# A graph network kernel on one core: first ranked segment of 6 chunks instead of 8, and node rows loaded behind the given rows

## The chip, the cores and the metric

The kernel runs on 1 core of one Trainium2 chip. The metric is the device time of one execution, in microseconds (us): the median of the runs of a kernel. Engines are named as in the profile: PE (matmul), DVE (VectorE), ACT (ScalarE), POOL (GpSimd), SP (SyncE). SPq, ACTq and POOLq are the DMA-issuing instructions of an engine.

## The reference

Four message-passing layers over one graph of 3125 nodes with 160 features and 100000 edges. Each layer normalises the node rows, gathers one node row per edge, multiplies it with edge weights from a small network on the edge's attributes, and sums the products per node; a dense stage per node follows. In outline:

```python
edge_index = jnp.stack([src, dst])
h = jnp.maximum(_layernorm(x, axis=-1), 0.0)
x = x + _L0_gnn_ref(h, edge_attr_3, edge_attr_64, ..., edge_index)   # gathers h[dst], sums per src
h = jnp.maximum(_layernorm(x, axis=-1), 0.0)
x = x + _L1_gnn_ref(h, node_vec1, src, dst, edge_attr_4, edge_attr_10, ...)  # gathers h[src], sums per dst
...
return x
```

Layer 0 sums over `src`, which arrives unsorted, so the edges have to be brought into bins of `src` first. Layers 1 to 3 sum over `dst`, which arrives sorted. Everything that the change touches lies in this ordering stage ahead of layer 0.

## The kernel before

**What the ordering stage does.** The edges lie as 128 partitions by 782 columns, cut into 34 chunks of 23 columns. `src` falls into 100 bins of 32 nodes. Each edge needs a slot of `rows_dram[0]` (tiles of 128 edges, each within one bin). The stage has these parts:

- *Init.* ACT issues one DMA (`rows_a<-acc`, line 997) that fills the whole of `rows_dram[0]` with blank rows; it signals `s_init`. POOL waits for it ahead of its first scatter (line 787), SP ahead of the rows below (line 596).
- *Count and rank, on DVE and PE.* `count(0)` marks each of the 100 bins over all 782 columns and PE sums the marks; `bases(0)` makes each column's base. `rank(o, lo, hi)` then makes, for the columns lo to hi, one mark per bin (line 1261), two matmuls on PE (lines 1814 to 1817) and one predicated copy on DVE (line 1400). `positions` turns the ranks into slots (lines 1410 to 1415) and signals `s_pos[0]`. Ranking runs in three segments, `SEGMENTS = (0, 8, 18, 34)` in chunks: segment 0, then `vectors(1, ...)` (unit vectors of the columns behind segment 0; those of segment 0 are made within `count(0)`), `tiles(0)`, segment 1, `count(1)`, `bases(1)`, `tiles(1)` (whose end is line 1375, `s_out_rows`), `turn_keys`, segment 2 and two halves of `rank(1)`. The statistics of the node rows wait for `s_nodes` behind all of that.
- *Scatter, on POOL.* For each chunk, 23 indirect DMAs (line 794), one per column, write one edge row per partition to its slot. A chunk needs its rows staged in one of two buffers (`stage_rows`, SP, line 572, waits until the scatter two chunks earlier has landed) and filled by ACT (`fill`, lines 1040 to 1046: vector, index, key, slot).
- *Given rows.* The second set of edge attributes goes in given order from DRAM through SBUF, where ACT adds two columns (`complete`, lines 1010 and 1012), back to DRAM (`given`, SP, lines 579 and 583), 34 chunks through two buffers. SP does 35 steps of it: a step loads chunk c and stores chunk c-1.

**The order of SP's queue** is written by hand and is what the change edits: key and vector loads, `stage_rows` 0 and 1, the node rows `x` and `attr` (lines 587 and 590, signal `s_nodes`), the `src` keys a second time (lines 593, 595), the wait for `s_init`, then 11 steps of `given`, `stage_rows(2)`, and `GIVEN_EACH` = 4 steps between each later `stage_rows` up to chunk 7, then the steps that are left. Behind these: a wait for `s_out_rows`, five small tables written out (lines 669 to 673), a wait for the given rows' stores, `tile_starts` written, waited for and read back (lines 679 to 681), and only then `stage_rows` of the first chunk of segment 1:

```python
sp.dma_start(starts_dram[:, :], starts_row[0:1, :]).then_inc(s_blocks, 16)
sp.wait_ge(s_blocks, 16)
sp.dma_start(block_at[0:ROW_GROUPS, :], ...).then_inc(s_blocks, 16)
...
for c in range(SEGMENTS[1], CHUNKS):
    stage_rows(c, c // 2, c % 2)
```

**The order of ACT's queue** follows it: fills of the chunks of segment 0 with 10 and then `GIVEN_EACH` `complete`s between them, after `roots(1)`, the square roots of `vectors(1, ...)`.

Behind the last scatter the edge stage of layer 0 begins: SP waits for `s_scat`, DVE for `s_placed`.

Of the kernel before, what the change touches and what calls it, by code (L numbers as in the profile page):

```python
# [16 lines left out]
P = 128  # L17
# [3 lines left out]
BLOCKS = -(-NODES // P)  # L21
# [13 lines left out]
CHUNKS = COLS // CHUNK  # L35
# [16 lines left out]
ENDS = (0, 6, 12, 18, 22, BLOCKS)  # L52
R2, R3 = math.sqrt(2.0), math.sqrt(3.0)
assert COLS % CHUNK == 0 and CHUNKS % 2 == 0 and GROUPS % 2 == 0
SEGMENTS = (0, 8, 18, CHUNKS)
BLOCKS_FROM = 10
BLOCK_LANES = 64
BLOCK_STEPS = GT * (P // BLOCK_LANES)
GIVEN_FIRST, GIVEN_EACH = 10, 4
assert BLOCKS_FROM >= SEGMENTS[1] + 2 and BLOCKS_FROM % 2 == 0 and BLOCKS_FROM + BLOCK_STEPS + 2 <= CHUNKS  # L60
assert GIVEN_FIRST + GIVEN_EACH * (SEGMENTS[1] - 2) == CHUNKS
ROW_GROUPS = TCOLS * P // GT
# [4 lines left out]
assert WORK >= 2 * PRODS * 416 + 2 * 512  # L67
PREP_FROM = SEGMENTS[2]
VEC_CUTS = (0, SEGMENTS[1] * CHUNK, COLS)
PAD_STEP = NODES // (P * GT)  # L70
# [17 lines left out]
def within(v, n):  # L88

    return not is_static(v) or 0 <= v < n  # L90
# [9 lines left out]
def wait(eng, signal, value):  # L100

    if is_static(value) and value <= 0:
        return
    if isinstance(signal, Signal):
        eng.wait_ge(signal.sem, value + signal.base)
    else:
        eng.wait_ge(signal, value)
# [127 lines left out]
def gnn_program(nc, t):  # L235

    ctx = ExitStack()
    with ctx:
        def sb(name, shape, dt=F32):
            return ctx.enter_context(nc.sbuf_tensor(name, shape, dt))  # L240

        def sem(name):
            return ctx.enter_context(nc.semaphore(name))
# [15 lines left out]
        x = sb("x", [P, BLOCKS * NF])  # L259
        attr = sb("attr", [P, BLOCKS])  # L260
# [131 lines left out]
        s_nodes = sem("s_nodes")  # L392
# [149 lines left out]
        def block_buffer():  # L542

            return gath_flat[0:ROW_GROUPS, 0:BLOCK_LANES * B_W]

        def pair_record(kind, i):

            _, record = nc.values_load_multi_w_load_instructions(
                guide[0:1, bass.ds(i * RECORD, RECORD)], engines=(kind,), min_val=0, max_val=COLS - 1,
                skip_runtime_bounds_check_because="bins and columns of tiles")  # L550
            bins = [nc.s_assert_within(v, 0, BINS - 1, skip_runtime_bounds_check_because="bins") for v in record[0:2]]
            return bins + list(record[2:4])
# [9 lines left out]
        def _(sp):  # L562
# [5 lines left out]
            def stage_rows(c, half, q):  # L568

                wait(sp, s_scat[q], half * (16 * CHUNK))  # L570
                sp.sem_inc(s_apart["sp"], 1)
                sp.dma_start(stage[0][q], t["rows_a"][:, bass.ds(c * (CHUNK * A_W), CHUNK * A_W)]).then_inc(s_stage[0][q], 16)

            def given(c, half, q):

                if within(c, CHUNKS):
                    wait(sp, s_given[q], half * 16)
                    sp.sem_inc(s_apart["sp"], 1)
                    sp.dma_start(stage[1][q], t["rows_b"][:, bass.ds(c * (CHUNK * B_W), CHUNK * B_W)]).then_inc(s_stage[1][q], 16)
                if within(c - 1, CHUNKS):  # L580
                    wait(sp, s_fill[1], c * 2)
                    sp.sem_inc(s_apart["sp"], 1)
                    sp.dma_start(given_dram[0:P * COLS, :].rearrange("(p c) w -> p (c w)", p=P)[:, bass.ds((c - 1) * (CHUNK * B_W), CHUNK * B_W)],
                                 stage[1][1 - q]).then_inc(s_given[1 - q], 16)
            for c in range(2):
                stage_rows(c, 0, c)
            sp.dma_start(x[:, :].rearrange("p (j c) -> p j c", j=BLOCKS),
                         t["x"].rearrange("(j p) c -> p j c", p=P)).then_inc(s_nodes, 16)
            with nc.allow_non_contiguous_dma(reason="one word per node"):
                sp.dma_start(attr[:, :], t["node_vec1"].rearrange("(j p) c -> p (j c)", p=P)).then_inc(s_nodes, 16)  # L590

            whole = COLS // P * P
            sp.dma_start(flat_keys[:, 0:whole].bitcast(I32).rearrange("p (b e) -> p b e", e=P),
# [3 lines left out]
            step = 0  # L597
            for c in range(2, SEGMENTS[1]):
                for _ in range(GIVEN_FIRST + 1 if c == 2 else GIVEN_EACH):
# [2 lines left out]
                stage_rows(c, c // 2, c % 2)  # L602
            for step in range(step, CHUNKS + 1):
                given(step, step // 2, step % 2)

            def tables(n, parts):

                S, m = s_p[n], BLOCKS // STORES
                for i in parts:
                    wait(sp, S["h"] if n == 2 else S["tab"], m * (i + 1))  # L610
                    sp.dma_start(table_dram[n].rearrange("(j p) c -> p j c", p=P)[:, m * i:m * (i + 1), :],
                                 table[:, m * i * NF:m * (i + 1) * NF].rearrange("p (j c) -> p j c", j=m)).then_inc(S["td"].sem, 16)
# [70 lines left out]
            def store_block(i):  # L683
# [3 lines left out]
                             block_buffer().rearrange("g (l c) -> g l c", c=B_W)).then_inc(s_copy, 16)  # L687
            for c in range(SEGMENTS[1], CHUNKS):
                stage_rows(c, c // 2, c % 2)
# [37 lines left out]
        def _(pool):  # L727
# [88 lines left out]
            for q in range(2):  # L816
                pool.wait_ge(s_scat[q], 16 * CHUNK * (CHUNKS // 2))

            pool.wait_ge(s_copy, 16 * BLOCK_STEPS)
            pool.wait_ge(s_flag, 1)  # L820
            _, (flag,) = nc.values_load_multi_w_load_instructions(
                unsorted[0:1, 0:1], engines=(POOL,), min_val=0, max_val=P * COLS,
                skip_runtime_bounds_check_because="a count of edges")
            with pool.If(flag != 0):
# [27 lines left out]
                with pool.Fori(0, TCOLS * P // GT) as c:  # L852
                    _, start = nc.values_load_multi_w_load_instructions(
                        starts_row[0:1, bass.ds(c * GT, GT)], engines=(POOL,),
                        min_val=0, max_val=P * COLS, skip_runtime_bounds_check_because="clamped to the number of edges")
                    for w in range(GT):
                        pool.dma_start(tiles_b[:, bass.ds(c, 1), w, :], sorted_dram[bass.ds(start[w], P), :].unsqueeze(1)).then_inc(s_gd, 16)
                    pool.wait_ge(s_gd, c * (16 * GT) + (ordered + 16 * GT))
                    pool.sem_inc(s_apart["pool"], 1)
# [1220 lines left out]
```

## Time and profile before

| what | us |
|---|---|
| median of 3 runs | 5577.6 (5576.04 to 5580.81) |
| the profiled execution, its own time | 5567.3 |
| its span in the trace | 5564.6 |
| POOL busy over the span | 4003.2 (72%) |
| DVE busy | 3534.9 (64%) |
| PE busy | 4312.1 (77%) |

Times in the trace count from the start of the span. Of the profiled execution 2.7 us lie outside its span. "Idle before" an instruction is followed by what released it; 0.30 us with the releaser "issue" is the gap between two instructions of one engine that wait for nothing. In a timeline row the columns are start, duration, engine, line, operation, operands, count, and in brackets the idle time before it.

### The profile page before, as it was taken

Reading aid. Unit: us, or ns where it says so; the run is one execution under the profiler, and the core shown is the slowest. Engines: PE = TensorE matmul, PEld = TensorE weight load, DVE = VectorE, ACT = ScalarE, POOL = GpSimd, SP = SyncE. Lnnn points to the kernel's source line nnn. Section 1 sums busy time; section 2 is a strip of 40 time slices with the busy share of each in tenths; the row PEclk is TensorE's granted clock in tenths of the full one; section 3 lists DMA queues with packets and bytes.
Section 4 is the critical chain, followed back from the end, with each engine's and each line's share of the span. In section 5 each row is a group of like instructions: output and inputs, shape, how many; then the busy total and the mean of one; then the engine's idle time right before and its main releaser. Section 6 shows DMA issues by size and latency. Waiting matters only on the chain.

```text
span 5564.6 us, 105356 instructions
## 1 busy us (share of the span) xinstructions
PE 4312.1 (77%) x24426; PEld 3347.2 (60%) x24426; DVE 3534.9 (64%) x11475; ACT 3407.4 (61%) x14606; POOL 4003.2 (72%) x4336
## 2 busy tenths in 40 slices
PE   7796112089999999889999997555566788889998
PEld 5553011067777777777888886444444576667777
DVE  8896000177777777667778887333333477778888
ACT  0000000056666666378899997677788778888896
POOL 5777777777777777377777775777777557777775
PEclk9898555599999999999999998555555699999999
DMA  9624553144444444133333331333333223333332
GB/s 317 183 82 105 126 121 89 53 90 95 94 93 94 94 94 92 28 81 80 81 81 82 83 82 53 81 79 82 80 81 82 63 63 81 80 82 82 82 83 52
DMA packets 632977, 504.27 MB, mean 91 GB/s; under 512 B 424231, under 2 KB 538342, under 8 KB 630455
## 3 DMA queue, kind: packets, MB, share of 16 engines
q0 software_dynamic: 183824, 307.52, 22.0%
q1 hardware_dynamic: 430566, 156.52, 12.2%
q10 hardware_dynamic: 17984, 33.56, 1.6%
q8 instruction: 212, 3.47, 0.3%
q14 instruction: 391, 3.20, 0.2%
HBM read 400.41 MB, written 96.88 MB: 89 GB/s over the span
## 4 chain that ended last, share of the span: by engine, by line
POOL 29%; issue 22%; PE 22%; DVE 4%; DMA 2%; POOLq 1%; DVEq 1%; ACT 0%; SPq 0%; ACTq 0%
POOL gath L961 24%; PE bank L1948 6%; PE bank L1922 4%; POOL gath L939 4%; PE bank L1950 4%; PE bank L1998 2%; PE bank L1990 1%; DVE acc L1529 1%; PE bank L1944 1%; PE bank L1892 1%; DMA gath<-table,acc 1%; DMA gath<-table,rows 1%; DVE work L1563 1%; POOLq L952 1%; DVE work L1545 0%
## 5 line engine op out<-in xcount | busy, mean ns | idle before, releaser
L961 POOL DMA_INDIRECT gath<-table,acc x2346 | 2223.5, 948 | 763.9 <-issue 691.2
L1121 ACT ACTIVATE sel<-acc,rows 128x32 f32<-128x32 f32 x10560 | 2293.0, 307 | 434.2 <-DVE acc L1520 431.0
L1529 DVE TENSOR_TENSOR acc<-acc,bank 128x160 f32 (+1 forms) x3520 | 1213.5, 345 | 942.3 <-PE bank L1944 561.8
L1948 PE MATMUL bank<-work,sel 128*128 128x160 f32 (+1 forms) x5280 | 1400.2, 347 | 116.3 <-DVE acc L1529 111.6
L1950 PE MATMUL bank<-work,sel 128*128 128x160 f32 x5280 | 1154.4, 300 | 0.0
L1948 PEld LDWEIGHTS bank<-work,sel 128*128 128x128 f32 x5280 | 838.6, 190 | 401.0 <-issue 382.9
L939 POOL DMA_INDIRECT gath<-table,rows x880 | 840.4, 955 | 278.4 <-issue 247.7
L1922 PE MATMUL bank<-w,work 64*128 64x224 f32 (+2 forms) x5280 | 921.1, 369 | 49.2 <-DVE work L1545 42.7
L794 POOL DMA_INDIRECT rows_a<-acc x782 | 754.5, 965 | 281.8 <-issue 237.8
L1950 PEld LDWEIGHTS bank<-work,sel 128*128 128x128 f32 x5280 | 913.2, 191 | 45.8
L1944 PE MATMUL bank<-gath,sel 128*128 x1760 | 566.3, 496 | 411.3 <-POOLq L947 357.1
L1944 PEld LDWEIGHTS bank<-gath,sel 128*128 128x128 f32 x1760 | 442.3, 315 | 535.2 <-issue 517.7
L1922 PEld LDWEIGHTS bank<-w,work 64*128 64x128 f32 (+1 forms) x5280 | 558.7, 188 | 311.8 <-issue 234.8
L1542 DVE TENSOR_TENSOR work<-bank,gath 128x128 f32<-128x128 f32 x1760 | 503.1, 286 | 212.5 <-POOLq L947 131.3
L1545 DVE TENSOR_TENSOR work<-bank,gath 128x192 f32<-128x192 f32 x1760 | 610.0, 347 | 4.0 <-issue 3.1
L1121 ACT ACTIVATE sel<-sel,rows 128x32 f32<-128x32 f32 x2640 | 581.8, 309 | 43.4 <-DVE sel L1520 41.4
L1040 ACT ACTIVATE acc<-acc 128x69 f32 (+1 forms) x34 | 9.3, 272 | 850.9 <-DMA acc<-in_rows_a 768.1
L1105 ACT ACTIVATE work<-bank 128x512 f32<-128x512 f32 (+1 forms) x330 | 241.8, 733 | 272.0 <-PE bank L1892 232.6
L1563 DVE TENSOR_TENSOR work<-bank,gath 128x288 f32<-128x288 f32 x880 | 356.8, 447 | 0.0
L1817 PE MATMUL bank<-acc,ident 100*128 100x391 f32 (+3 forms) x1000 | 346.6, 438 | 0.0
L1745 PE MATMUL bank<-ident,sel 128*64 128x128 f32 x25 | 10.2, 408 | 404.1 <-ACT sel L1023 404.1
L1559 DVE TENSOR_TENSOR work<-bank,gath 128x256 f32<-128x256 f32 x440 | 184.9, 420 | 152.1 <-POOLq L927 137.9
(288 smaller groups left out, 3646.7 us busy)
## 6 DMA issues: line engine op xcount, KB each, us to landing
rows<-rows_b SPq DMA_DIRECT2D x330, 128.0 KB
gath<-table,acc POOLq DMA_INDIRECT x2346
rows_a<-acc ACTq DMA_DIRECT2D x1, 30360.0 KB, 103.6
rows<-rows_a SPq DMA_DIRECT2D x110, 256.0 KB
acc<-in_rows_a SPq DMA_DIRECT2D x34, 793.5 KB, 7.3
rows_b<-gath SPq DMA_DIRECT2D x16, 896.0 KB, 10.5
gath<-table,rows POOLq DMA_INDIRECT x880
acc<-in_rows_b SPq DMA_DIRECT2D x34, 368.0 KB, 3.7
```

The costliest lines, as they stand in the source:

```text
L794: pool.indirect_dma_start(rows_dram[0][:, :], bass.IndirectOffsetOnAxis(ap=pos_r[q][:, u:u + 1], axis=0), stage[0][q][:, u * A_W:(u + 1) * ...
L939: pool.indirect_dma_start(gath[q][:, u, :], None, table_dram[n][:, :], bass.IndirectOffsetOnAxis(ap=at, axis=0)).then_inc(S[f"gt{k % LANES ...
L961: pool.indirect_dma_start(gath_all[:, u, :], None, table_dram[n][:, :], bass.IndirectOffsetOnAxis(ap=index[:, k:k + 1], axis=0)).then_inc( ...
L1121: i = act.activation(sel[q][:, t, at:at + BIN], hot, ACT.Copy, scale=e[:, k:k + 1])
L1529: dve.tensor_tensor(sums, sums, bank(6 + b, P, 256 * h, 256 * h + L.width), ALU.add).then_inc(S["fl"].sem, 1)
L1542: dve.tensor_tensor(ps, wt[:, 0:128].rearrange("p (w c) -> p w c", w=2), one[:, 0:S0].unsqueeze(1).to_broadcast([P, 2, S0]), ALU.mult)
L1545: ins = dve.tensor_tensor(pv, wt[:, 128:L.wcols].rearrange("p (w m) -> p w m", w=nv) .unsqueeze(2).to_broadcast([P, nv, 3, V1]), one[:, S0 ...
L1563: ins = dve.tensor_tensor(pv, wt[:, h, 128:L.wcols].rearrange("p (w m) -> p w m", w=nv) .unsqueeze(2).to_broadcast([P, nv, 3, V1]), two[:, ...
L1922: ins = pe.matmul(bank(at_bank, P, first, first + L.wcols), hid, w, start=True, stop=True, skip_group_check=True)
L1944: ins = pe.matmul(out, sel[qv][:, t, 0:128], ring_column(columns[h]), start=True, stop=True, skip_group_check=True)
L1948: pe.matmul(out, sel[qv][:, t, 96:224], work[:, a + NF:a + NF + L.width], start=True, stop=False, skip_group_check=True)
L1950: ins = pe.matmul(bank(6 + b, P, 256 * h, 256 * h + NF), sel[qv][:, t, 0:128], work[:, a:a + NF], start=False, stop=True, skip_group_check ...
```

## The change

The first segment has 6 chunks instead of 8 and the second 12 instead of 10. `GIVEN_EACH` becomes 6, so that all 34 `complete`s still fit between the fills of segment 0. The two loads of node rows move from the head of SP's queue to behind the last step of `given`.

```diff
-SEGMENTS = (0, 8, 18, CHUNKS)
+SEGMENTS = (0, 6, 18, CHUNKS)
-GIVEN_FIRST, GIVEN_EACH = 10, 4
+GIVEN_FIRST, GIVEN_EACH = 10, 6
@@ sync engine
             for c in range(2):
                 stage_rows(c, 0, c)
-            sp.dma_start(x[:, :].rearrange("p (j c) -> p j c", j=BLOCKS),
-                         t["x"].rearrange("(j p) c -> p j c", p=P)).then_inc(s_nodes, 16)
-            with nc.allow_non_contiguous_dma(reason="one word per node"):
-                sp.dma_start(attr[:, :], t["node_vec1"].rearrange("(j p) c -> p (j c)", p=P)).then_inc(s_nodes, 16)
...
             for step in range(step, CHUNKS + 1):
                 given(step, step // 2, step % 2)
+            sp.dma_start(x[:, :].rearrange("p (j c) -> p j c", j=BLOCKS),
+                         t["x"].rearrange("(j p) c -> p j c", p=P)).then_inc(s_nodes, 16)
+            with nc.allow_non_contiguous_dma(reason="one word per node"):
+                sp.dma_start(attr[:, :], t["node_vec1"].rearrange("(j p) c -> p (j c)", p=P)).then_inc(s_nodes, 16)
```

## Rows read from the trace of the kernel before

**Rows 1.** Windows by stage; PE, PEld, DVE, ACT, POOL busy, PEclk, DMA share, GB/s.
```profile
107.60:1120.20 1012.60, 426.80 (x1702) 262.41 (x1702) 413.97 (x1116) 49.78 (x248) 769.57 (x798) 0.67 0.43 110
```

**Rows 2.** Waits of POOL, 0 to 1150 us: total, times, longest.
```profile
POOL rows_a L794 <- issue: 237.8, 780, 0.3
POOL rows_a L794 <- ACT acc L1046: 43.7, 1, 43.7
```

**Rows 3.** Timeline of POOL: first scatter, first of chunk 6, first of chunk 8.
```profile
107.60 1.26 POOL L794 DMA_INDIRECT rows_a<-acc  x1 [43.66 <-ACT acc L1046]
...
286.07 0.96 POOL L794 DMA_INDIRECT rows_a<-acc  x1 [0.30 <-issue]
...
344.56 0.96 POOL L794 DMA_INDIRECT rows_a<-acc  x1 [0.31 <-issue]
```

**Rows 4.** DMA issues, 0 to 120 us: count, KB each, us to landing.
```profile
rows_a<-acc ACTq DMA_DIRECT2D x1, 30360.0 KB, 103.6
```

**Rows 5.** Timeline of ACT: init DMA, fill of chunk 0, roots(1), fills of chunks 4, 8.
```profile
2.86 0.58 ACTq L997 DMA_DIRECT2D rows_a<-acc  x1
...
106.01 0.27 ACT L1040 ACTIVATE acc<-acc 128x69 f32<-128x69 f32 x1 [82.80 <-DVE acc L1415]
...
109.99 0.70 ACT L1002 ACTIVATE acc<-acc 128x598 f32<-128x598 f32 x1 [2.90 <-DVE acc L1273]
...
207.16 0.27 ACT L1040 ACTIVATE acc<-acc 128x69 f32<-128x69 f32 x1 [8.83 <-DMA acc<-in_rows_a]
...
321.59 0.21 ACT L1046 ACTIVATE acc<-acc 128x23 int32 x1
```

**Rows 6.** DMA queues, 16 to 41 us: packets, MB, share of 16 engines.
```profile
q10 hardware_dynamic: 3302, 7.29, 73.7%
q1 hardware_dynamic: 3300, 2.06, 26.0%
```

**Rows 7.** The same, 42 to 59 us: SP's queue (q10 has 2825 too).
```profile
q1 hardware_dynamic: 2825, 0.01, 9.9%
```

**Rows 8.** The same, 68 to 100 us.
```profile
q10 hardware_dynamic: 5522, 12.19, 105.8%
```

**Rows 9.** Windows: the 100 bins of segment 0, those of segment 1.
```profile
54.13:103.93 49.80, 48.38 (x304) 35.56 (x304) 47.81 (x201) 0.00 (x0) 7.63 (x15) 0.97 1.03 371
125.89:180.60 54.71, 52.89 (x300) 37.39 (x300) 52.75 (x200) 4.03 (x24) 41.59 (x44) 0.96 0.64 187
```

**Rows 10.** Timeline of SP's queue: node rows, then given rows, then chunks 2 to 8.
```profile
4.87 0.53 SPq L587 DMA_DIRECT2D x<-in_x  x1
5.44 24.32 SPq L590 DMA_DIRECT2D attr<-in_node_vec  x1
29.80 18.70 SPq L593 DMA_DIRECT2D side<-in_skey  x1
...
106.52 0.84 SPq L579 DMA_DIRECT2D acc<-in_rows_b  x2
...
157.59 0.37 SPq L572 DMA_DIRECT2D acc<-in_rows_a  x1
...
178.26 0.34 SPq L572 DMA_DIRECT2D acc<-in_rows_a  x1
...
199.93 0.87 SPq L572 DMA_DIRECT2D acc<-in_rows_a  x1
...
301.84 4.37 SPq L583 DMA_DIRECT2D rows_given<-acc  x2
...
316.23 117.19 SPq L572 DMA_DIRECT2D acc<-in_rows_a  x5
```

**Rows 11.** Timeline of DVE: end of tiles(1), s_out_rows.
```profile
247.25 0.42 DVE L1375 TENSOR_SCALAR acc<-acc 1x196 int32<-1x196 int32 x1
```

**Rows 12.** DMA, 5528 to 5531 us: one store of 640-byte rows alone, GB/s in 40 slices.
```profile
GB/s 0 34 196 316 375 341 375 350 333 384 367 333 375 350 367 367 358 358 375 333 188 43 17 17 0 0 0 0 0 0 0 0 0 0 0 0 0 0 0 0
```

**Rows 13.** DMA queues, 308 to 312 us: packets, MB, share of 16 engines.
```profile
q1 hardware_dynamic: 792, 0.02, 10.0%
```

## The prediction

> **What bounds the kernel now.** I read the windows by stage first. The change touches only the first 1120 us; behind them the same program runs as before. In the stage from 107.6 to 1120.2 us POOL is busy for 770 of 1013 us and everything else far less [rows 1]. The waits of POOL say why that is the bound: its scatters were never late. 780 of the 782 scatters show only the fixed gap of 0.30 us, and one wait, of 43.7 us, stands ahead of the first [rows 2]. So the stage is "start of the first scatter, plus 1012 us of POOL", and the edge stage of layer 0 waits for its end. Two things can move the time: the start at 107.60 us, and any chunk that comes to POOL late [rows 3]. There the reader is to see also where chunk 6, the first one behind the new segment 0, begins (286.07), and chunk 8, the first one behind the old (344.56).
>
> **What sets the start.** Two chains end at the same moment. The init DMA is issued at 2.86 us and lands 103.6 us later, at 106.5 [rows 4, 5]; SP's first given rows go out at 106.52, just behind it [rows 10]. DVE has the positions of segment 0 at 105.8, ACT's fill begins at 106.01 and ends at 106.6 [rows 5]. POOL starts 1.0 us behind the later one. Each half of the change shortens one of the two chains, so they have to be costed together.
>
> **The init chain.** While x loads, the init's queue (q10) and SP's (q1) move packets one to one: 3302 and 3300 in 25 us, or 132 per us each [rows 6]. With nothing beside it the init moves 5522 in 32 us, 172.6 per us [rows 8]. The 3200 rows of x take 24.2 us at 132 per us, and cost the init 24.2 x (1 - 132/172.6) = 5.7 us. While attr loads (3200 packets of one word, 2825 in 17 us, 166 per us, 19.3 us in all) the init loses 19.3 x (1 - 166.2/172.6) = 0.7 us [rows 7]. Without both it lands 6.4 us earlier, at 100.1.
>
> **The DVE chain.** The 100 bins of segment 0 take 49.8 us at 184 columns, those of segment 1 54.7 at 230, DVE being busy for 96% of both [rows 9]. The trace has no 138 columns; carried on by the same step of 46 columns that is 44.9, 4.9 us less (bounds: nothing, if the pitch of a bin had its floor at 184 columns, and 12.5, if the time went with the columns; I take the step, being the nearest rows). The unit vectors of 138 columns instead of 184 inside count(0) and the shorter position steps save an estimated 1.1 us. Positions stand at 99.8, the fill's end at 100.6. Segment 1 has 276 columns instead of 230 and gives the 4.9 us back; tiles(1) still ends near 248 us [rows 11], which is early enough for everything below.
>
> POOL therefore starts at 101.5, **6.1 us earlier**. If nothing came late that would be the whole result.
>
> **The supply of chunks 2 to 6.** Here the same edit adds to SP's queue. Its waits let the order count: 11 given steps take from 106.52 to 157.59, then chunk 2 is staged; 4 steps and a stage take 20.7, then 21.7 us, so a step is 5.1 us [rows 10]. All of this moves with the init, plus 0.7 us, since roots(1), which now has two chunks' more vectors and a start later against the init, holds the first complete [rows 5]. With 6 steps between stages: chunk 2 is staged at 100.1 + 0.7 + 51.1 = 151.9, chunk 3 at 182.8 (20.7 + 10.2 later), chunk 4 at 214.7 and chunk 5 at 246.6 (31.9 each). From a staging to the start that it allows pass 7.5 to 8.8 us: chunk 4, staged at 199.93, was filled from 207.16 for 0.6 us [rows 5, 10], and POOL takes its 1.0. POOL wants them at 161, 191, 221 and 251 us: its six chunks ahead of chunk 6 took 178.5 us [rows 3], 29.7 each. Chunks 4 and 5 come late by some 2 us each; a cycle of 31.9 us can't feed a chunk of 29.7. POOL would want chunk 6 at 284.3: of the 6.1 us gained about 4 are gone by then.
>
> **Chunk 6 is the large term.** It isn't staged within the given rows but behind them and behind tile_starts, as chunk 8 was. Before, the pair of given stores that ended the stream was through SP's queue at 306.2, the last of them issued at 305.8, and chunk 8's rows at 316.23, so 10.4 us lie between: the tables, the landing of tile_starts and its way back [rows 10]. Its fill ended at 321.8 [rows 5], while POOL wanted it at 344.6 [rows 3]: 22.8 us to spare, which hid all of it. Now two chunks less stand ahead of it, 58 us of POOL, and the given rows end only 29 us earlier, at 246.6 + 30.3 = 276.9 (6 steps). Behind them come x and attr, and tile_starts lands behind both, being on the same queue.
>
> What x and attr cost there the trace doesn't show, since they ran beside the init. x: 640-byte rows alone move at about 355 GB/s [rows 12], which gives 5.8 us for 2.05 MB [rows 6]; beside the init it took 24.2; I take 6, the nearer case, with nothing but scatters beside it. attr: from below, 1.7 us, the 9.9% share of 17 us that its packets held of the engines [rows 7]; from above, 19.3 us, its pace one to one with the init. The nearest row is the store of the two-word records, 792 packets in 4 us on a queue that was else nearly idle [rows 13]: 16.2 us for 3200. That one has other gaps in it (three issues one behind another), so I take 11, between it and the pace at which 640-byte rows run (5.8). The 24.32 us that attr's issue took before [rows 10] I take for the queue being full beside the init, not for work of SP: x's packets moved at 132 per us then, and 24.32 us of that are its 3200.
>
> The Trainium skill ("DMA: Bandwidth & Descriptors", the fit in "Anatomy of one DMA") prices a DMA at 2.0 us plus bytes over 436 GB/s, by size alone. By that fit x would be 6.7 us and attr 2.0, and the sum 8 us smaller than mine. That the pair's drain depends on attr's count of packets is what I set against it; no row of before shows attr alone.
>
> **Sum.** Chunk 6 staged at 276.9 + 10.4 + 6 + 11 = 304.3; filled 5.6 us later, started after 1.0 more: 310.9. Before it started at 286.07. Net **+24.8 us**, with a stall of 26.6 us at chunk 6 that swallows the gain at the front and the two small stalls. Chunk 7 is staged right behind 6; from chunk 8 on a stage waits for the scatter two chunks back and has a whole chunk's time, as before. The 782 scatters themselves, the gathers between them and all that follows keep their time. Against the profiled execution that is 5567.3 + 24.8 = 5592.1; the median of the runs stands 10.3 us above it, so 5602.4.
>
> At nothing I cost the wait of statistics for s_nodes: x and attr land near 300 us, and DVE comes to it beyond 500 us. If that cover were gone it would delay the table of layer 0, not the scatters.
>
> **Rivals.**
> - *Small packets are cheap.* attr takes its lower bound, 1.7 us, and chunk 6 is 9.3 us earlier: +15.5, 5593. For it: the packets hardly slowed the init. Against it: the records' pace. Chance 0.22. The skill's fit says the same (+16 or so).
> - *SP itself is held.* The 24.32 us of attr and the 18.70 us of the issue behind it [rows 10] are SP's own work in making descriptors, not a full queue. Then the tables go out 43 us later instead of 17 and the sum is +51, 5628. Against it: x, with as many packets, was issued in 0.53 us. Chance 0.06.
> - *The supply keeps up* (the faster side). The place is the given stream: if a given step took 4.3 us or less instead of 5.1, the 34 steps up to the last store would save 27 us, chunk 6 would be ready when wanted, and 6.1 us would stay: 5571. It decides from a staging of chunk 6 at 277 us or before, which is where I put the end of the given rows, without the 27 us behind it. For it: the first steps run ahead of the scatters' full load, and the loads alone land in less. Against it: a step waits for a store to land and for ACT, so each costs its latency whatever runs beside it, and the first eleven took 51.1 us [rows 10], 4.6 each, with no stage between them. Chance 0.04.
> - *Both ends kind*: a pace of 4.9 and a cheap attr give +9, 5587, within 0.2%. Chance 0.09.
> - My forecast, attr at 6 to 19 us: 0.59.
>
> **Numbers.** 0.2% is 11 us, about what a measurement of this kernel can tell from no change. The range takes attr from 1.7 to 19.3 us (+15.5 to +33) and 2 to 3 us for the pace of the given steps on either side, and a little of the held SP: 5589 to 5615. Slower by over 0.2%: 0.59 + 0.22 + 0.06 less a little, 0.86; within 0.10; faster 0.04.
>
> **What the next profile would show.** Right: the first scatter at about 101.5 us; the init landing near 100; small waits of POOL ahead of chunks 4 and 5 and one of 20 to 35 us ahead of chunk 6, then none; the last scatter at about 1144 us; behind it nothing changed. In SP's queue the last given store near 277 and the first staging of segment 1 near 304. Wrong: no wait at chunk 6 (the queue is faster than I read it), a first scatter still at 107 (a third chain holds it), or a change behind 1120 us.

## The result and the profile after

| | before | after |
|---|---|---|
| median, 6 runs each (us) | 5577.9 (5576.0 to 5580.8) | 5612.6 (5610.0 to 5613.6) |
| the profiled execution, its own time | 5567.3 | 5610.0 |
| its span | 5564.6 | 5608.4 |
| first scatter | 107.6 | 125.2 |
| first scatter of chunk 6 | 286.1 | 321.1 |
| first scatter of the last chunk | 1091.4 | 1128.3 |

The change makes the kernel 34.7 us slower, a ratio of 1.0061 (1.0049 to 1.0072). The forecast was 5602.4 with a range of 5589 to 5615. In two of the five sets of runs below every execution, those of the kernel before among them, took about 7800 us for a reason that no run shows; up to the end of segment 0 their traces run as the others do (in the segments alone the first scatter is at 125.0 there and at 124.8 in the other set), and the argument uses only that part of them.

The two profiled executions differ by 43.8 us in span: 37.3 up to the end of the scatters, and 6.5 behind it, where the program is the same and single executions of the kernel before already differ by up to 13.5 us (5567.3 to 5580.8).

The first view is again the windows by stage, of the kernel after: the 100 bins of segment 0, and the stage from the first scatter to the last (columns as in [rows 1]).

```profile
53.44:120.80 67.36, 66.95 (x299) 59.43 (x300) 46.93 (x200) 0.00 (x0) 7.49 (x15) 0.50 0.72 261
125.20:1157.50 1032.30, 437.43 (x1702) 262.28 (x1702) 425.52 (x1116) 50.06 (x248) 773.49 (x798) 0.67 0.43 109
```

The stage of the scatters is 20 us longer than before (1032 for 1013 us in [rows 1]), and it starts 17.6 us later. Segment 0, which has a quarter fewer columns, takes 67.4 us where it took 49.8 [rows 9]: PE is busy for 66.95 of the 67.36 us, DVE no longer is, and the granted clock is 0.50 throughout where it was 0.97. That row is what the forecast didn't see.

The waits of POOL in the kernel after, 0 to 1180 us, and its timeline at chunks 0, 5 and 6, answer to [rows 2, 3].

```profile
POOL rows_a L794 <- issue: 236.9, 777, 0.5
POOL rows_a L794 <- ACT acc L1046: 74.8, 4, 58.4
```

```profile
125.21 1.41 POOL L794 DMA_INDIRECT rows_a<-acc  x1 [58.43 <-ACT acc L1046]
...
276.69 1.41 POOL L794 DMA_INDIRECT rows_a<-acc  x1 [0.95 <-ACT acc L1046]
...
321.11 0.96 POOL L794 DMA_INDIRECT rows_a<-acc  x1 [15.10 <-ACT acc L1046]
```

So two places carry the loss: chunk 6, as forecast, though its wait is 15.1 us and not 26.6, and the start, which was to be 6 us earlier and is 17.6 later. Behind chunk 6 come 1.9 us more by the last chunk. Chunk 5 was late by 0.95 us, and a fourth wait holds the 0.3 that are left of the 74.8.

SP's queue of the kernel after answers to [rows 10].

```profile
101.22 0.82 SPq L579 DMA_DIRECT2D acc<-in_rows_b  x2
128.96 0.34 SPq L583 DMA_DIRECT2D rows_given<-acc  x1
...
172.52 0.37 SPq L572 DMA_DIRECT2D acc<-in_rows_a  x1
...
205.86 0.35 SPq L572 DMA_DIRECT2D acc<-in_rows_a  x1
...
236.92 0.37 SPq L572 DMA_DIRECT2D acc<-in_rows_a  x1
...
267.71 0.37 SPq L572 DMA_DIRECT2D acc<-in_rows_a  x1
...
293.80 4.37 SPq L583 DMA_DIRECT2D rows_given<-acc  x2
298.21 0.43 SPq L601 DMA_DIRECT2D x<-in_x  x1
298.69 6.77 SPq L604 DMA_DIRECT2D attr<-in_node_vec  x1
...
312.16 0.23 SPq L679 DMA_DIRECT2D tile_starts<-acc  x1
314.84 0.31 SPq L681 DMA_DIRECT2D acc<-tile_starts  x1
315.28 0.85 SPq L572 DMA_DIRECT2D acc<-in_rows_a  x2
```

And the DMA issues, the first row of 0 to 125 us, the others of 297 to 315 us (KB each, us from issue to landing):

```profile
rows_a<-acc ACTq DMA_DIRECT2D x1, 30360.0 KB, 98.3
```

```profile
x<-in_x SPq DMA_DIRECT2D x1, 2000.0 KB, 10.7
...
attr<-in_node_vec SPq DMA_DIRECT2D x1, 12.5 KB, 12.2
```

Three things stand in them. The init lands after 98.3 us, not 103.6: the first given rows go out at 101.2, 5.3 us earlier, where 6.4 were forecast. But the first of them is stored only at 128.96, since ACT's `complete` stands behind `roots(1)`, which waits for segment 0. And attr's issue takes 6.8 us, not 24.3. x lands 10.7 us after its issue, at 308.9, and attr 12.2 us after its own, at 310.9.

**Where the clock went.** Windows of the stretch around the start of the ranking, first of the kernel before, then of the kernel after. From 49 to 53 us PE has almost nothing to do, as it waits for DVE's bases; 58 to 100 is ranking.

```profile
49.00:53.00 4.00, 0.82 (x6) 0.36 (x4) 2.85 (x8) 0.00 (x0) 1.60 (x4) 1.00 1.09 376
53.00:58.00 5.00, 3.46 (x14) 2.87 (x15) 3.79 (x15) 0.00 (x0) 2.51 (x5) 0.67 1.09 374
58.00:100.00 42.00, 41.74 (x272) 30.38 (x271) 41.66 (x177) 0.00 (x0) 5.12 (x11) 1.00 1.06 384
```

```profile
49.00:53.00 4.00, 0.34 (x2) 0.25 (x2) 3.36 (x9) 0.00 (x0) 3.21 (x7) 1.00 1.04 367
53.00:58.00 5.00, 4.15 (x20) 3.73 (x20) 3.71 (x17) 0.00 (x0) 0.00 (x0) 0.52 1.05 378
58.00:100.00 42.00, 42.00 (x189) 37.27 (x188) 29.65 (x125) 0.00 (x0) 7.49 (x15) 0.50 0.99 358
```

Both kernels lose the full clock (2.4 GHz) just behind that pause. Before, it is at half from 54.7 to 58.1 us and comes back. After, it is at half (1.2 GHz) from 53.2 to 148.8 us: through the whole of segment 0, although PE is busy for 42.00 of 42 us, and through the pause of 17.6 us behind it. It comes back 4.0 us after segment 1, with its 276 columns, begins on PE:

```profile
139.79 3.14 PE L1794 MATMUL bank<-ident,acc 128*1 128x128 f32 x14 [17.64 <-DVE acc L1339]
144.82 0.41 PE L1816 MATMUL bank<-work,acc 128*128 128x276 bf16 x1 [1.89 <-DVE work L1261]
```

The groups of PE by shape between 60 and 95 us, line 1817 in the kernel before and in the kernel after, give the price of a matmul (busy us, mean ns; neighbours overlap, so the busy time is less than count times mean):

```profile
L1817 PE MATMUL bank<-acc,ident 100*128 100x184 f32 x152 | 35.2, 334 | 0.0
```

```profile
L1817 PE MATMUL bank<-acc,ident 100*128 100x138 f32 x106 | 35.9, 486 | 0.0
```

With fewer columns the matmul takes 486 ns for 334. In DVE's timeline of the kernel after, the copies now stand 0.67 us apart, each waiting for PE (before they stood 0.47 apart with no wait):

```profile
95.12 0.32 DVE L1400 COPY_PREDICATED acc<-work,bank 128x138 f32<-128x138 int16 x1 [0.20 <-PE bank L1817]
95.33 0.25 DVE L1261 TENSOR_SCALAR work<-acc,iota_bins 128x138 bf16<-128x138 bf16 x1
95.79 0.32 DVE L1400 COPY_PREDICATED acc<-work,bank 128x138 f32<-128x138 int16 x1 [0.20 <-PE bank L1817]
```

A hundred bins of 0.67 us are the 67 us of segment 0. Behind the scatters nothing changed: 4420 us from just behind their end, after and then before, hold the same work to within 1%.

```profile
1150.00:5570.00 4420.00, 3765.72 (x21997) 2991.51 (x21998) 2992.47 (x9929) 3347.38 (x14299) 3167.64 (x3417) 0.88 0.33 80
```

```profile
1113.00:5533.00 4420.00, 3779.09 (x22053) 3007.04 (x22054) 2998.60 (x9955) 3346.18 (x14312) 3163.84 (x3419) 0.88 0.33 80
```

### The profile page after: what moved, and what is told of

It reads as the page before. It is cut to its first block, busy times and chain, and to the rows that moved or that the text cites. A ratio compares the mean times of both kernels' runs of the same rounds, so it can differ in the third digit from the quotient of the medians.

```text
span 5608.4 us, 105367 instructions
## 1 busy us (share of the span) xinstructions
PE 4333.8 (77%) x24426; PEld 3361.4 (60%) x24426; DVE 3546.1 (63%) x11475; ACT 3412.2 (61%) x14606; POOL 4015.8 (72%) x4336
## 3 DMA queue, kind: packets, MB, share of 16 engines
q1 hardware_dynamic: 430566, 156.52, 12.2%
## 4 chain that ended last, share of the span: by engine, by line
POOL 29%; issue 22%; PE 20%; DVE 5%; DMA 1%; DVEq 1%; POOLq 1%; SPq 0%; ACT 0%; ACTq 0%
POOL gath L961 24%; PE bank L1948 6%; POOL gath L939 4%; PE bank L1922 4%; PE bank L1950 4%; PE bank L1998 2%; DVE acc L1529 2%; PE bank L1990 1%; PE bank L1944 1%; DMA gath<-table,acc 1%; PE bank L1892 1%; DVE work L1563 1%; DVE work L1545 1%; DVE work L1542 1%; POOLq L952 1%
## 5 line engine op out<-in xcount | busy, mean ns | idle before, releaser
L1817 PE MATMUL bank<-acc,ident 100*128 100x391 f32 (+3 forms) x1000 | 375.6, 473 | 0.0
L1745 PE MATMUL bank<-ident,sel 128*64 128x128 f32 x25 | 10.2, 406 | 411.3 <-ACT sel L1023 411.3
## 6 DMA issues: line engine op xcount, KB each, us to landing
rows_a<-acc ACTq DMA_DIRECT2D x1, 30360.0 KB, 98.3
```

## The experiments

Three questions. Which half of the change costs what? Why is the clock at half in segment 0: because its bins are now too narrow in themselves (W), or because the pause takes the clock away and something has to bring it back (B)? And if B, what brings it back? Last: with both causes mended, is there a faster kernel?

### The two halves alone

The segments alone: the kernel after, with the two loads of node rows back at the head of SP's queue.

```diff
@@ sync engine, kernel after
                 stage_rows(c, 0, c)
+            sp.dma_start(x[:, :]..., t["x"]...).then_inc(s_nodes, 16)
+            sp.dma_start(attr[:, :], t["node_vec1"]...).then_inc(s_nodes, 16)
...
                 given(step, step // 2, step % 2)
-            sp.dma_start(x[:, :]..., t["x"]...).then_inc(s_nodes, 16)
-            sp.dma_start(attr[:, :], t["node_vec1"]...).then_inc(s_nodes, 16)
```

> The change without its second part: SEGMENTS (0, 6, 18) and 6 given steps between stagings, node rows loaded at the head of SP's queue as before. Theory W (the narrow rank): 138 columns a bin leave PE too little to do, its granted clock falls to half at the end of count(0) and stays there, so segment 0 takes 67 us as in the changed kernel, first scatter at 125 us, the init's landing (106) hidden behind it. Chunk 6 is staged 10.4 us behind the last given store instead of 17.5, so 7 us less than the changed kernel: 5605 us. Rival P (the clock's fall is due to the node rows' move or to chance): clock back to full within a few us as before, first scatter at 107.6, chunk 6 at about 300: 5592 us.

> The kernel of e1_segments_only again, for its time on a chip on which the kernel before takes about 5570 us. x and attr at the head of SP's queue, so chunk 6 is staged 10.4 us behind the last given store and not 17.5: 7 us less than the changed kernel's +34.7, +28 against before, 1.0050. First scatter at 125 as in the changed kernel. Rival: x and attr cost nothing behind the given rows, +35.

The first of these runs belongs to a 7800-us set: 7839.8 against 7813.7 us, 1.0026 (1.0003 to 1.0049), with the clock at half from 52.8 to 148.4 us and the first scatter at 125.0. The second: 5604.5 against 5581.3, **1.0039 (1.0025 to 1.0053), +23 us** where 28 were expected. The clock is at half from 52.5 to 148.1 and the first scatter at 124.8. So the late start belongs to the segments alone and has nothing to do with the loads. In its SP queue the last given store ends at 292.9 and chunk 6 is staged 9.2 us behind it; POOL waits 4.8 us for chunk 6, where the kernel after waits 15.1. Of the 13.2 us by which chunk 6 is staged earlier than there the loads explain 7.9. The other 5.3 come from the given rows, which end that much earlier here (292.9 against 298.2); the expected 28 didn't have them, and no run explains them.

```profile
288.43 4.50 SPq L583 DMA_DIRECT2D rows_given<-acc  x2
292.98 0.81 SPq L669 DMA_DIRECT2D tile_guide<-acc  x1
...
302.12 5.94 SPq L572 DMA_DIRECT2D acc<-in_rows_a  x2
```

The move alone: the kernel after with the old segments.

```diff
-SEGMENTS = (0, 6, 18, CHUNKS)
+SEGMENTS = (0, 8, 18, CHUNKS)
-GIVEN_FIRST, GIVEN_EACH = 10, 6
+GIVEN_FIRST, GIVEN_EACH = 10, 4
```

> The other part alone: node rows behind the given rows, SEGMENTS (0, 8, 18) and 4 given steps as before. Theory W: segment 0 at 184 columns keeps its clock, positions at 105.8, so DVE's chain holds the first scatter at 107 although the init lands at 101. Chunk 8 had 22.8 us to spare and x and attr cost 7 of them: no wait. 5577 us, within 0.1% of before. Rival P: the clock stays at half once the node rows are gone from the head, segment 0 takes 80 us or more, first scatter beyond 135: 5605 us.

> The kernel of e2_move_only again, for its time on such a chip. Init lands at 101 instead of 106.5, but DVE's chain holds the first scatter at 107 to 108; x and attr lie behind the given rows, where chunk 8 had 22.8 us to spare: no change, within 1 us of before. Rival: up to 5 us faster, if the init alone held the start.

7824.6 against 7813.7 us, 0.9998 (0.9971 to 1.0024), in the 7800-us set, and 5580.7 against 5581.3, **0.9999 (0.9989 to 1.0008)**, in the other. The init lands earlier and gains nothing, since segment 0 with its 184 columns holds the first scatter (at 109.0; in the first run 108.1); the 8.7 us that the loads add behind the given rows are hidden in the 22.8 to spare at chunk 8. The end of the given stores at 306.4 and the first staging at 325.11 are 18.7 us apart, for 10.0 before [rows 10]: that is the price of x and attr there, 8.7 us. The last chunk's first scatter is 3.4 us later than before (1094.9), which the time doesn't show. In both runs the clock comes back after some 7 us, though PE pauses as it does in the kernel after.

### Width or pause

Bridging the pause: the kernel after, with 14 matmuls of 128 columns on PE ahead of its wait for the totals and 5 behind the small matmul that follows, into a bank that nothing reads. The bins stay at 138 columns.

```diff
@@ tensor engine, bases(0)
+                if o == 0:
+                    for _ in range(14):
+                        pe.matmul(bank(3, P, 0, P), ident[:, :], tri, start=True, stop=True, ...)
                 pe.wait_ge(s_total, o + 1)
                 pe.matmul(bank(2, BINS, 0, 1), ...).then_inc(s_first, 1)
+                if o == 0:
+                    for _ in range(5):
+                        pe.matmul(bank(3, P, 0, P), ident[:, :], tri, start=True, stop=True, ...)
```

> The changed kernel with 14 matmuls (128x128 f32, result unused) on PE while it waits for bases(0), and 5 behind the first-slot product: PE has no pause before segment 0. Theory W: full clock to about 54 us, and it falls all the same within segment 0, since the bins are as narrow: segment 0 over 60 us, first scatter at 115 to 125, time 5605 to 5613. Rival B (the pause alone is to blame; at 138 columns a clock that never fell stays up): full clock through segment 0, 45 us for it, first scatter at 102, chunk 6 at about 301, 5592 us.

> The kernel of e3_bridge_pause again, for its time on a chip on which the kernel before takes about 5570 us. From e3 (first scatter at 103.0, clock full through segment 0) and from the changed kernel (17.5 us between last given store and chunk 6's staging): given rows end near 274, chunk 6 is staged near 292 and starts near 298 where POOL wants it at 281.5: +12 us against before, 1.0021. Rival: with the start mended chunk 6 is no longer late, and the time is 4 us below before.

The first run (7813.9 against 7813.7 us, 0.9999, 0.9975 to 1.0022) showed the clock at full from 16.7 to 98.7 us and the first scatter at 103.0. The second: 5577.0 against 5570.7, **1.0014 (1.0005 to 1.0024), +6.3 us** where 12 were expected, since the given rows end at 269.0 and not near 274; the clock is at full from 14.1 to 99.5. Its windows over the same three stretches, and its waits of POOL:

```profile
49.00:53.00 4.00, 3.58 (x33) 3.38 (x31) 3.36 (x12) 0.00 (x0) 0.25 (x1) 1.00 1.05 369
53.00:58.00 5.00, 4.82 (x41) 4.41 (x41) 4.97 (x25) 0.00 (x0) 2.23 (x5) 1.00 1.04 379
58.00:100.00 42.00, 36.79 (x266) 29.14 (x264) 40.92 (x184) 1.08 (x8) 5.45 (x11) 0.99 0.98 357
```

```profile
POOL rows_a L794 <- DMA rows_a<-acc: 39.0, 2, 38.7
POOL rows_a L794 <- ACT acc L1046: 11.7, 1, 11.7
```

Theory W falls: bins of 138 columns hold the full clock perfectly well once they have it, with PE less busy than in the kernel after (36.8 of 42 us). Entered at half, they don't get it back in the six other traces with 138 columns. The bins take 42.7 us from the first matmul at 53.18 to the last copy at 95.84, DVE-bound, and POOL now waits for the init's landing (the releaser is the DMA `rows_a<-acc`), not for positions. What is left against the kernel before is the wait of 11.7 us at chunk 6.

### What brings the clock back

More work per bin: the kernel after, with one more matmul of 64 columns, with weights of its own, behind each bin of segment 0.

```diff
@@ tensor engine, rank
                               start=False, stop=True).then_inc(s_prefix, 1)
+                    if o == 0 and lo == 0:
+                        pe.matmul(bank(3, P, 0, 64), ident[:, :], tri[:, 0:64], start=True, stop=True, ...)
```

> The changed kernel with one more matmul per bin of segment 0 (128x128 by 64 columns f32, result unused), so that PE has as much to stream per bin as at 184 columns; the pause stays. Theory W: the clock falls in the pause and comes back within some 4 us as in the kernel before, a bin takes 0.42 to 0.45 us, first scatter at 102 to 104, chunk 6 at about 301 us since x and attr and the given rows hold it: 5592 us. Rival B or P: half clock stays, the added matmul costs 0.2 us more per bin, first scatter at 145, time 5632 us.

The expectation that the clock would come back was wrong: 7872.2 against 7813.7 us, 1.0072 (1.0045 to 1.0099). The clock stays at half from 53.0 to 182.7 us, and the first scatter moves out to 156.7. Its window from 58 to 100 us has PE and its weight loads both at 42.00 of 42 us:

```profile
58.00:100.00 42.00, 42.00 (x212) 42.00 (x212) 19.83 (x85) 0.00 (x0) 3.55 (x8) 0.50 0.99 357
```

Wider matmuls: the kernel after, in which PE alone ranks 184 columns in segment 0. DVE still marks and copies 138, and what PE computes beyond them is read by nobody.

```diff
-            def rank(o, lo, hi):
+            def rank(o, lo, hi, wide=0):
 
+                hi += wide
...
-            pe.wait_ge(s_base[0], 1)
-            rank(0, 0, SEGMENTS[1] * CHUNK)
+            pe.wait_ge(s_base[0], 2)
+            rank(0, 0, SEGMENTS[1] * CHUNK, 2 * CHUNK)
```

> The changed kernel with PE ranking 184 columns in segment 0 as before the change, while DVE marks and copies 138 (PE streams 46 columns more per matmul, results unused; it starts one base later). The pause stays. Theory C (what counts for the clock's return is how much PE streams per bin without more weight loads): clock at half at 53, full again some 4 to 7 us later, first scatter at 103 to 104. Rival D (it is DVE's shorter work or the instant of the fall): clock stays at half, a bin takes PE 0.83 us, first scatter at 138 or later. Chunk 6 late as in the changed kernel under both: under C chunk 6 at about 298, 5590 us on a chip like that of the first profiles.

7789.8 against 7797.8 us, 0.9985 (0.9962 to 1.0008), in the 7800-us sets, so only its segment 0 is read. There the clock is at half for 3.4 us (54.0 to 57.4) and then full, as in the kernel before; the first scatter is at 102.8.

```profile
58.00:100.00 42.00, 40.59 (x288) 34.95 (x285) 41.00 (x193) 0.00 (x0) 3.64 (x9) 1.00 0.99 357
```

So adding a third more columns to the matmuls that are there, with no further weight load, makes the ranking *faster* (DVE's marks and copies untouched). More instructions on the same engine don't do it. Where the pause is left as it was, the clock comes back within 3.4 to 6.8 us in all four traces in which PE ranks 184 columns (the kernel before, the move alone twice, this one), and not before the end of segment 0 in all six with 138 (the kernel after, the segments alone twice, the added matmul, and the supply alone, below, twice). The instant of the fall isn't what separates them: it falls at 52.9 to 54.7 us in the first group and at 50.8 to 53.2 in the second, 52.9 with 184 columns and 53.2 with 138 among them. What it is in the columns that decides, these runs don't say.

### Mending both

Supply alone: the kernel after, with chunks 6 and 7 staged and filled within the given rows again, though they belong to segment 1; ACT waits for their positions ahead of chunk 6.

```diff
+STAGED = 8
-GIVEN_FIRST, GIVEN_EACH = 10, 6
+GIVEN_FIRST, GIVEN_EACH = 10, 4
@@ sync engine
-            for c in range(2, SEGMENTS[1]):
+            for c in range(2, STAGED):
...
-            for c in range(SEGMENTS[1], CHUNKS):
+            for c in range(STAGED, CHUNKS):
@@ scalar engine
-            for c in range(SEGMENTS[1]):
+            for c in range(STAGED):
+                if c == SEGMENTS[1]:
+                    act.wait_ge(s_pos[0], 2)
                 fill(c, c // 2, c % 2)
...
-            act.wait_ge(s_pos[0], 2)
-            pairs(act, SEGMENTS[1], SEGMENTS[2], fill)
+            pairs(act, STAGED, SEGMENTS[2], fill)
```

> The changed kernel with only the supply mended: chunks 6 and 7 staged within the given rows, no bridging matmuls. Theory: segment 0 still at half clock, first scatter at 125 (17.6 later than before), no chunk late: 5595 on a chip like that of the first profiles, 17 us better than the changed kernel. Rival: chunk 6 was late because of POOL or ACT and not of its place in SP's queue: still a wait of some 15 us there, 5612.

> The kernel of e6_early_only again, for its time on such a chip. First scatter at 125 (segment 0 at half clock), no wait of POOL at chunk 6: +17.6 us against before, 1.0032. Rival: a wait of some 15 us stays at chunk 6 or 8, and the time is that of the changed kernel, +34.7.

7804.1 against 7797.8 us, 0.9995 (0.9975 to 1.0014), in the 7800-us set; and 5588.4 against 5570.7, **1.0033 (1.0021 to 1.0046), +17.8 us**, with 17.6 expected: the late start and nothing else. The clock is at half from 51.9 to 147.4 us.

Both: this edit and the bridged pause together.

> The changed kernel with both faults taken out: the 19 bridging matmuls on PE around bases(0), so that its clock never falls before segment 0, and chunks 6 and 7 staged and filled within the given rows (4 steps between stagings as before the change; ACT waits for segment 1's positions ahead of chunk 6). Theory: first scatter at 103 instead of 107.6, no chunk late, x and attr hidden: 4.6 us faster than before, 5573 on a chip like that of the first profiles. Rival: the supply binds again somewhere (chunk 8 behind x and attr): a wait of POOL there and no gain.

> The kernel of e5_bridge_and_early again, to see whether the execution behind 125 us runs as in the first profiles (the kernel before at 5578 us) or as in the last seven runs (at 7800 us). Theory, on a chip like that of the first profiles: full clock through segment 0, first scatter at 103, no wait of POOL at chunk 6 or 8, 4.6 us faster than before: 5573 us. Rival: the supply of chunks binds somewhere and the gain is gone: 5578 us or more, with a wait of POOL to show for it.

7776.3 against 7797.8 us, 0.9975 (0.9955 to 0.9996), in the 7800-us set; and 5564.8 against 5569.7, **0.9990 (0.9981 to 1.0000), 4.9 us less than before**, with 4.6 expected. The waits of POOL, 0 to 1180 us, of the supply alone, and of both:

```profile
POOL rows_a L795 <- issue: 237.8, 780, 0.3
POOL rows_a L795 <- ACT acc L1047: 59.8, 1, 59.8
```

```profile
POOL rows_a L795 <- issue: 237.8, 780, 0.3
POOL rows_a L795 <- DMA rows_a<-acc: 34.7, 2, 34.4
```

In neither is a chunk late; in the second the first scatter (102.8 us) waits for the init's landing. That is 4.8 of the 6.1 us that the forecast saw at the front, kept to the end. The median is below both kernels', though 4.9 us lies inside the 0.2% (11 us) that the prediction took as what one measurement can tell from no change, and the interval touches 1. Whether the moved loads and a bridged pause would do as much with the old first segment of 8 chunks was not run, so these 4.9 us aren't shown to need the short segment.

The four kernels with the short first segment and the moved loads, against the kernel before:

| | supply as in the change | chunks 6, 7 within the given rows |
|---|---|---|
| pause as it was | +34.7 | +17.8 |
| pause bridged | +6.3 | −4.9 |

The shifts of the last chunk's first scatter in the four traces are +36.9, +17.3, +7.2 and −4.9 us (1128.3, 1108.7, 1098.6 and 1086.5 against 1091.4). The clock is worth 28 us in the change as it stands and 23 with the supply mended: it delays the first scatter and also the given rows, on which chunk 6 depends.

## Why the prediction was right, and where it was wrong

The direction, the total (5602.4 against 5612.6, within the range) and chunk 6 as a place of loss were right. But the start went the other way; two errors of opposite sign stand in the sum, and the larger was not among the mechanisms weighed.

| step | forecast | after | pause bridged |
|---|---|---|---|
| given rows go out behind the init | 100.1 | 101.2 | 102.2 |
| bins of segment 0 take | 44.9 | 67.4 | 42.7 |
| first scatter | 101.5 | 125.2 | 103.0 |
| last given store through SP | 276.9 | 298.2 | 269.0 |
| from there to the staging of chunk 6 | 27.4 | 17.1 | 18.7 |
| chunk 6 starts | 310.9 | 321.1 | 293.3 |
| its wait on POOL | 26.6 | 15.1 | 11.7 |

- **The init chain** was right: 98.3 us from issue to landing where 97.2 were forecast (100.1 less 2.9).
- **The DVE chain** was the step that failed: "carried on by the same step of 46 columns that is 44.9". The two rows that it rested on [rows 9] are both at a clock of 0.96 or 0.97, and both kept DVE the bound. Carrying on a trend in size assumes that the clock stays; the pause of PE ahead of segment 0 and the dip to half from 54.7 to 58.1 us stood in the trace of before and weren't read. The bounds given for this term (nothing to 12.5 us less) lay both on the side of a gain, and the truth was 17.6 us more. With the clock kept, the bins take 42.7 us, so the step is only 2.2 us off. Segment 1 was to give the time back and tiles(1) to end near 248 us: it ends at 276.8, and at 251.0 with the pause bridged, both ahead of the given rows' end, so it holds nothing.
- **The given chain** was said to move "with the init, plus 0.7 us, since roots(1)", with two chunks' more vectors, "holds the first complete". The link to roots(1) was right, its price was not: at half clock roots(1) ends 27 us behind the first given load, and the first store moves from 111.0 to 129.0. With the bridge roots(1) is done at 102.8 and the first complete waits for its load instead. From a staging to the next pass 33.3, 31.1 and 30.8 us, for 31.9 forecast. From the first load to the staging of chunk 2 pass 45.5 us in the kernel with the bridge, for 51.1, and from the first store 43.6 us in the kernel after, for 46.6 before. Why they are quicker than before wasn't tried.
- **x and attr** were sized at 17 us, and cost 8.7 in the move alone (18.7 less 10.0), 8.7 with the pause bridged, 7.9 between the change (17.1) and the segments alone (9.2). The rival that small packets are cheap is right on this term: attr, sized at 11 us, lands 2.0, 1.5 and 1.8 us behind x in the kernel after, the move alone and the bridged one. The records' pace [rows 13] was a poor neighbour. The Trainium skill ("DMA: Bandwidth & Descriptors", "Anatomy of one DMA") gives 2.0 us plus bytes over 436 GB/s, measured there for DMAs that GpSimd issues; these two are SP's. Worked out from it, the pair is an estimated 8.7 us. The added delay of 7.9 to 8.7 us agrees with that; the single landings don't (x 10.7 us after its issue, attr 12.2, for an estimated 6.7 and 2.0), which would fit each waiting for what stands ahead of it in the queue; no run has either alone.
- **The reading that attr's issue of 24.32 us is the queue being full, and not work of SP,** held: behind the given rows the same issue takes 6.77 us, and the two key loads that stood behind it are issued in 0.51 and 2.36 us for 18.70 and 8.13. The rival that SP itself is held falls.
- **The rival that the supply keeps up** did not come about: with the clock kept, chunk 6 is staged at 287.7 and is 11.7 us late; its deciding point was 277.

Between the forecast and the profile the start of chunk 6 differs by 10.2 us: +21.3 for the given rows' end, −10.3 for x, attr and the tables, −0.8 from staging to start. With the clock kept at full, in the bridged kernel, chunk 6 starts 17.6 us ahead of the forecast and the time is +6.3 us, below the range. That the forecast came out near is in this sense luck; that POOL's supply at chunk 6 costs something once two chunks less stand ahead of it is the part that was understood.

## What to carry to other kernels

Before making a stage smaller, read PE's granted clock around it, window by window, and note what PE did ahead of each fall; a trend over sizes is only good at one clock. Where PE pauses at the entry of a stage of small matmuls, a few matmuls that nobody reads (19 here, worth 28 us) or wider ones in the stage are worth a trial; here they were worth more than the work saved. And where a load is moved behind a stream, ask who next needs that queue: here the order of SP's queue, not any engine, made chunk 6 late.

## What the runs showed of the hardware that was not expected

- **A fully busy PE kept at half clock.** PE was busy for 66.95 of 67.36 us at 0.50 with matmuls of 138 columns (weights of 128 and 100 rows); the clock stayed at half for 95.6 us in all, a pause of 17.6 us included. The same stream holds 0.99 if PE enters it without a pause. The clock comes back within 3.4 to 6.8 us with 184 columns, and within 4.0 with the 276 of segment 1. Another 64 columns with a weight load of their own don't bring it back (PE and its weight loads both busy for 42.00 of 42 us). What decides stays open.
- **3200 loads of one word are cheap when alone.** Beside the init, attr's issue took 24.32 us and its packets an estimated 19.3 us (3200 at the 166 per us of [rows 7]); behind the given rows the issue takes 5.9 to 6.8 us, attr lands 1.5 to 2.0 us behind x, and both together delay what follows by 7.9 to 8.7 us.
